# V in memory of its own and transposed early, both experts behind the output projection, output transposes last

## What is computed

```python
def _L0_attn_ref(q_x, ln1_w, ...):                 # q_x = layernorm(x)
    xn = _ln(q_x, ln1_w, ln1_b)
    q, k, v = (heads(xn @ w + b) for w, b in ...)  # 16 heads of 16
    fq = jax.nn.elu(q) + 1.0
    fk = jax.nn.elu(k) + 1.0
    kv = jnp.einsum('bhnd,bhne->bnde', fk, v)      # per row, summed over heads
    qkv = jnp.einsum('bhnd,bnde->bhne', fq, kv)
    k_sum = fk.sum(axis=1)
    qk = jnp.einsum('bhnd,bnd->bhn', fq, k_sum)
    attn = qkv / (qk[..., None] + 1e-06)
    attn = attn.transpose(0, 2, 1, 3).reshape(b, n, c) @ wo + bo
    x = q_x + attn
    h = _ln(x, ln2_w, ln2_b)
    h = jax.nn.gelu(h @ fc_w + fc_b, approximate=False)
    return x + (h @ proj_w + proj_b)

def _L0_ffn_ref(x, gate_w, ...):                   # x = layernorm(...), 8 experts
    logits = x.mean(axis=1) @ gate_w.T + gate_b
    gates = softmax over the two largest logits of each batch
    expert_out = jax.nn.gelu(jnp.einsum('bsd,eod->beso', x, expert_w) + expert_b, approximate=False)
    return jnp.einsum('be,beso->bso', gates, expert_out)

x = x + _L0_attn_ref(_layernorm(x), ...)
x = x + _L0_ffn_ref(_layernorm(x), ...)
```

## Time and profile before

| | us |
|---|---|
| median of 3 runs | 1278.87 (1278.82 to 1278.89) |
| profiled execution | 1278.0 |
| its span in the trace | 1276.2 |
| PE busy | 1108.7 (87%) |
| PE loading weights | 816.2 (64%) |
| DVE busy | 782.9 (61%) |
| ACT busy | 530.4 (42%) |
| POOL busy | 190.8 (15%) |
| mean granted TensorE clock | 0.884 |

### The profile page before, as it was taken

The page is one execution under the profiler, slowest core; times in us unless marked ns, Lnnn a source line. Parts: engine busy times, 40 slices in busy tenths (PEclk is TensorE's granted clock), DMA queues, the critical chain, the costliest instruction groups (busy, mean ns, idle before and its releaser), DMA issues.

```text
span 1276.2 us, 22032 instructions
## 1 busy us (share of the span) xinstructions
PE 1108.7 (87%) x7272; PEld 816.2 (64%) x7272; DVE 782.9 (61%) x1692; ACT 530.4 (42%) x835; POOL 190.8 (15%) x113
## 2 busy tenths in 40 slices
PE   6646988979797989999997989999999989795946
PEld 3444766757575858686775758586767667583723
DVE  2465566565757586666756676766666674646333
ACT  2413443534444444536353454536363444231322
POOL 1011202020111212120301112121203012111000
PEclk9757897979797989989897989899897989797969
DMA  4966656383737475665737473656658374311013
GB/s 161 187 143 157 116 140 149 104 180 95 173 98 173 104 165 115 173 148 153 168 121 173 114 172 116 160 128 173 148 147 174 125 165 106 102 55 53 17 66 116
DMA packets 242518, 170.21 MB, mean 133 GB/s; under 512 B 177040, under 2 KB 218256, under 8 KB 240144
## 3 DMA queue, kind: packets, MB, share of 16 engines
q1 hardware_dynamic: 235792, 158.80, 52.3%
q10 hardware_dynamic: 6656, 10.50, 2.4%
HBM read 93.75 MB, written 75.50 MB: 133 GB/s over the span
## 4 chain that ended last, share of the span: by engine, by line
PE 48%; issue 23%; DVE 14%; ACT 7%; DMA 3%; SPq 2%; POOL 1%; DVEq 1%; ACTq 0%; POOLq 0%
PE pq L963 13%; PE pj L949 10%; PE ps L925 7%; PE pq L869 5%; PE pt L934 4%; PE pt L857 3%; DVE nd L727 2%; DVE acc L818 2%; DVE am L700 1%; DVE hn L631 1%; ACT am L513 1%; DVE stat L621 1%; DMA scratch_nd<-ot 1%; DMA ot<-scratch_v 1%; SPq L366 1%
## 5 line engine op out<-in xcount | busy, mean ns | idle before, releaser
L716 DVE TENSOR_TENSOR hidden<-xhT,hidden 128x512 fp32r<-128x512 f32 x128 | 96.6, 755 | 224.0 <-ACT hidden L541 224.0
L963 PE MATMUL pq<-hT,w_fc 128*128 128x512 f32 x768 | 225.4, 433 | 9.4 <-DVE hT L723 5.2
L540 ACT ACTIVATE xhT<-pq,col 128x512 f32<-128x512 f32 x128 | 88.0, 688 | 323.1 <-PE pq L963 322.9
L949 PE MATMUL pj<-w_pj,hidden 128*128 128x256 f32 x1536 | 214.1, 288 | 0.7 <-DVE hidden L716 0.7
L949 PEld LDWEIGHTS pj<-w_pj,hidden 128*128 128x128 f32 x1536 | 191.6, 189 | 18.6 <-issue 9.8
L925 PE MATMUL ps<-kq 48*128 48x128 f32 x1024 | 155.7, 436 | 24.0 <-DVE am L700 14.7
L963 PEld LDWEIGHTS pq<-hT,w_fc 128*128 128x128 f32 x768 | 149.0, 207 | 41.3 <-issue 7.7
L700 DVE TENSOR_TENSOR am<-ps,mask 128x512 f32<-128x512 f32 x256 | 164.1, 682 | 17.4 <-PE ps L925 17.1
L925 PEld LDWEIGHTS ps<-kq 48*128 48x128 f32 x1024 | 133.8, 329 | 61.1 <-issue 36.9
L869 PE MATMUL pq<-zT,w_e 128*128 (+1 forms) x256 | 119.4, 614 | 11.8 <-DMA b_e<-in_eb 7.3
L458 POOL TENSOR_TENSOR rs<-var,mhalf 128x4 f32<-128x4 f32 x16 | 18.1, 1132 | 571.2 <-DVE var L744 571.2
(11 more groups left out here) (117 smaller groups left out, 1399.3 us busy)
## 6 DMA issues: line engine op xcount, KB each, us to landing
kq<-scratch_q SPq DMA_DIRECT2D x192, 128.0 KB, 3.7
kq<-scratch_k SPq DMA_DIRECT2D x192, 128.0 KB, 4.5
scratch_q<-hidden SPq DMA_DIRECT2D x32, 512.0 KB, 4.6
scratch_k<-hidden SPq DMA_DIRECT2D x32, 512.0 KB, 6.1
scratch_nd<-ot SPq DMA_DIRECT2D x16, 1024.0 KB, 3.9
nd<-scratch_nd SPq DMA_DIRECT2D x48, 256.0 KB, 3.3
x_sb<-in_x SPq DMA_DIRECT2D x16, 512.0 KB, 4.7
scratch_v<-feat_v ACTq DMA_DIRECT2D x16, 512.0 KB, 2.8
```

Of the source, the lines that this page charges most:

```text
L540: nc.scalar.activation(gelub[:, u], pq[u][:, :], ACT.Gelu, bias=b_fc[:, m:m + 1])
L716: nc.vector.tensor_tensor(hidden[:, m % SLOTS, 1], gelub[:, u], hidden[:, m % SLOTS, 0].bitcast(f32), ALU.subtract).then_inc(S["rest_ready ...
L949: last = nc.tensor.matmul(pj[u][:, D * s:D * (s + 1)], hidden[:, m % SLOTS, a, lo:lo + P], w_pj[:, b, m], start=False, stop=end)
L963: last = nc.tensor.matmul(pq[m % 2][:, :], w_fc[:, b, c, P * m:P * (m + 1)], hT[:, a, c], start=(n == 0), stop=(n == len(order) - 1))
```

## The change

- V is loaded into `vd`, a buffer of its own of 128 partitions, in which partition 8d + 2j + b holds dimension d of block (j, b). `VL` no longer waits for the store of `ot`; it waits until PE has read the last V, and stands second among SP's loads of a pass. To make room, `x2_sb` has one slot in place of two.
- V's transposes are 8 of 128 x 128 in place of 16 with 64 rows, and `VT` stands ahead of `N`, `D2` and `A2` in the pass.
- `F1` moves from ahead of `N` to behind `R`, next to `F3`. The DVE part of the second expert becomes a stage `F4` behind `H`; `FX` follows it.
- `F2` stands last in the pass, behind `B9`, and its transposes go into `pj`. `JA`, which empties `pj`, moves from the end of the pass to right behind `J7`.
- `E` moves behind `J7` in a full pass. The matmuls of zeros are gone: the first real matmul into each `pj` bank starts the accumulation.

```diff
-X2RING = 2
+X2RING = 1
...
-FULL = ["L", "XS", "M1", "K0", "J2", "Y", "M2", "DS", "M3", "Z", "D1", "M4", "VL", "XL", "X", "E", "J7", "F1", "N", "D2", "K1", "A2", "F3",
-        "FX", "R", "VT", "F2", "B0", "H", "B9", "JA"]
-HEAD = ["L", "XS", "M1", "K0", "J2", "Y", "M2", "DS", "M3", "Z", "D1", "M4", "VL", "XL", "E", "X", "J7", "G", "N", "D2", "K1", "F1", "A2",
-        "F3", "FX", "R", "VT", "F2", "B0", "H", "B9", "JA"]
+FULL = ["L", "XS", "M1", "VL", "K0", "J2", "Y", "M2", "DS", "M3", "Z", "D1", "M4", "XL", "X", "J7", "JA", "E", "VT", "N", "D2", "K1", "A2",
+        "R", "F1", "F3", "B0", "H", "F4", "FX", "B9", "F2"]
+HEAD = ["L", "XS", "M1", "VL", "K0", "J2", "Y", "M2", "DS", "M3", "Z", "D1", "M4", "XL", "E", "X", "J7", "JA", "G", "VT", "N", "D2", "K1", "A2",
+        "R", "F1", "F3", "B0", "H", "F4", "FX", "B9", "F2"]
...
-    stages(["XS", "C1", "J2", "C2", "Z", "C3", "C4", "XL", "J7", "E", "F1", "F3", "FX", "F2", "JA"], 18, [])
+    stages(["XS", "C1", "J2", "C2", "Z", "C3", "C4", "XL", "J7", "JA", "E", "F1", "F3", "F4", "FX", "F2"], 18, [])
...
+        vd = sb("vd", [P, H * HALF])
-        vd = ot
...
                 if p.stage == "VL":
                     wait("v_out", at("v_out"))
-                    wait("nd_out", at("nd_out"))
+                    for u in range(2):
+                        wait(f"pt_full{u}", at(f"pt_full{u}"))
...
-                if p.stage == "F3":
+                if p.stage == "F4":
                     for m in range(NC):
 
-                        wait(f"pq_free{m}", at(f"pq_free{m}", 1))
+                        wait(f"pq_free{m}", at(f"pq_free{m}"))
                         wait("acc_ready", at("acc_ready", m))
...
                 if p.stage == "VT":
                     wait("v_in", at("v_in"))
-                    rows, n = vd[0:NQ * HD].rearrange("p h t -> p (h t)"), NQ * HD
                     for u in range(2):
                         wait(f"pt_free{u}", at(f"pt_free{u}"))
-                        pe.sem_inc(held, 1)
-                        for g in range(HG):
-                            group = rows[:, P * HG * u + g:P * HG * (u + 1):HG]
-                            last = nc.tensor.transpose(pt[u][:, n * g:n * (g + 1)], group, ident[0:n, 0:n])
+                        for g in range(HG // 2):
+                            last = nc.tensor.transpose(pt[u][:, P * g:P * (g + 1)], vd[:, HG // 2 * u + g::HG], ident[:, :])
                         last.then_inc(S[f"pt_full{u}"], 1)
...
-                            nc.tensor.matmul(pj[u][:, :], zero[:, :], zero[:, :].unsqueeze(1).broadcast_to([1, 4, P]), start=True, stop=False)
...
-                                                        start=False, stop=end)
+                                                        start=(m == 0 and n == 0 and s == 0), stop=end)
...
                 if p.stage == "F2":
                     wait("acc_ready", at("acc_ready"))
                     for u in range(2):
-                        wait(f"pt_free{u}", at(f"pt_free{u}"))
+                        wait(f"pj_free{u}", at(f"pj_free{u}"))
```

More of the change, by code:

```diff
@@ L74 @@
 INC = {
[L75 to L78, removed]
+    "pt_full0": {"W1": 1, "WS": 1, "X": 1, "D2": 1, "VT": 1, "H": 1, "G": 1},
+    "pt_free0": {"W1": 1, "WS": 1, "X": 1, "D2": 1, "VT": 1, "H": 1, "G": 1, **rounds("pt_free0")},
+    "pt_full1": {"X": 1, "D2": 1, "VT": 1, "H": 1},
+    "pt_free1": {"X": 1, "D2": 1, "VT": 1, "H": 1, **rounds("pt_free1")},
     "pq_full0": {"D2": 1, "F1": 1, "F3": 1, **rounds("pq_full0")},
@@ L102 @@
     "pool_ready": {"G": 1}, "logit_ready": {"G": 1}, "gexp_ready": {"G": 1}, "gate_ready": {"G": 1},
-    "acc_ready": {"P": 1, "F1": 2, "F3": 2},
+    "acc_ready": {"P": 1, "F1": 2, "F4": 2},
     "out_stored": {"P": 16, "F2": 16},
@@ L161, in walk @@
     late = ["XS", "J2", "Z", "E"]
-    last = ["XL", "F1", "F3", "FX", "F2"]
+    last = ["XL", "F1", "F3", "F4", "FX", "F2"]
     def without(names, *out):
@@ L407, in run @@
                     for u in range(2):
-                        wait(f"pt_free{u}", at(f"pt_free{u}", 1))
+                        wait(f"pj_free{u}", at(f"pj_free{u}", 1))
                     sp.dma_start(out_t[p.t], out_sb[:, :, :]).then_inc(S["out_stored"], 16)
@@ L418, in _ @@
             nc.gpsimd.memset(mhalf[:, :], -0.5).then_inc(const_done, 1)
-            nc.gpsimd.memset(vd[:, :, :], 0.0).then_inc(const_done, 1)
+            nc.gpsimd.memset(vd[:, :], 0.0).then_inc(const_done, 1)
             nc.gpsimd.memset(vb[:, :, :], 1.0).then_inc(const_done, 1)
@@ L520, in run @@
                         wait(f"pt_full{u}", at(f"pt_full{u}", 1))
[L521 to L522 removed]
+                        src = pt[u][:, :].rearrange("p (g d j) -> p j g d", d=HD, j=2 * NQ)
+                        dst = vb[:, :, :].rearrange("p (j g) e -> p j g e", j=2 * NQ)[:, :, HG // 2 * u:HG // 2 * (u + 1), 0:HD]
                         nc.scalar.activation(dst, src, ACT.Identity).then_inc(S[f"pt_free{u}"], 1)
@@ L832, in run @@
                     for u in range(2):
-                        wait(f"pt_full{u}", at(f"pt_full{u}", 1))
+                        wait(f"pj_full{u}", at(f"pj_full{u}", 1))
                         o = out_sb[:, 2 * u:2 * u + 2]
-                        nc.vector.tensor_tensor(o, pt[u][:, :].rearrange("p (s d) -> p s d", d=D), o,
-                                                ALU.add).then_inc(S[f"pt_free{u}"], 1)
+                        nc.vector.tensor_tensor(o, pj[u][:, :].rearrange("p (s d) -> p s d", d=D), o,
+                                                ALU.add).then_inc(S[f"pj_free{u}"], 1)
             walk(dve, run)
@@ L845, in _ @@
                 pe.wait_ge(w_in[n], 16)
+            features_copied = []
             def run(p):
@@ L896, in run @@
                     transposes(xhat)
+                    features_copied[:] = [at(f"pt_free{c}", 1) for c in range(NC)]
                 if p.stage == "D2":
-                    copied(0)
+                    for c in range(NC):
+                        wait(f"pt_free{c}", features_copied[c])
                     for j in (4, 5, 0, 1, 2, 3):
@@ L1051, in run @@
                                 lo = P * (2 * u + s)
-                                last = nc.tensor.transpose(pt[u][:, D * s + P * m:D * s + P * (m + 1)],
+                                last = nc.tensor.transpose(pj[u][:, D * s + P * m:D * s + P * (m + 1)],
                                                            acc[:, m, lo:lo + P], ident[:, :])
-                        last.then_inc(S[f"pt_full{u}"], 1)
+                        last.then_inc(S[f"pj_full{u}"], 1)
             walk(pe, run)
```

12 lines of the change are left out of this document (5 added, 7 removed).

## The result

The changed kernel takes 1286.3 us (median of four runs, 1284.61 to 1286.83) against 1278.88 (1278.82 to 1279.81): 1.0059 times, with a 95% interval of 1.0043 to 1.0076. It is slower by 0.6%. Two later comparisons of the same pair gave 1.0079 [1.0061, 1.0096] and 1.0066 [1.0041, 1.009]. The predicted time was 1287.

A forecast was written before the change was run, and what follows sets the result against it. PE bounds the rounds, a DVE chain the end of a pass. Full passes +11.2, gate +1.6, early -4.1, passes 16 and 17 +1.4, pass 18 -1.8 sum to +8.3 us: 1287 predicted, range 1271 to 1297; slower had 0.62.

The forecast's parts named there:

- Start of N: DVE's reciprocal and split, bound in full passes by the landing of `nd`: 6.36 us after I, a gain of 0.26.
- I: The first issue of the loads of `nd` in a pass, from which the prediction counts its times.
- the mark (I + 5.4): Sign of being wrong: DVE's N starting 5.4 us after I with `out_sb`'s load behind the `nd` loads.
- N to the end of `hn`: DVE's stretch from reciprocal to `hn`, without an expert in it: 20.68 us, as in an early pass.
- `hn` to U: From `hn` to the next pass's first product (U): 5.2 us on DVE, then 2.0 of output transposes; 4.04 before.
- Passes with the gate: Three passes where the addition `JA` delays the gate's sum on DVE: +0.5 us each, +1.6 together.
- The rounds: PE-bound stretch of a pass: without the matmuls of zeros 0.53 us less; V's earlier loads make nothing wait.
- Early passes and tail: Five early passes, `nd` landing at 5.4: -4.1 us; passes 16 and 17: +1.4; pass 18: -1.8.
- the clock holds: Faster rival: PE's clock stays at 1.00 through the end of a pass, 21 us less, 1266; chance 0.10.
- The rule of the Trainium skill: Transposes don't count as PE-busy like matmuls; low stretch begins as now, ends later: sum +14, time 1292.
- Cancelling: No-change rival: output transposes at the high clock, or `nd` landing at 4.3; either gives 1275 to 1279; chance 0.15.
- The wait for V: Faster rival: half of ACT's 29.3 us of waits behind V's load set the end: sum -6.4, 1272; chance 0.13.

## Why the prediction was right

**How near.** The mechanism and the sign were right. That 1287 stands so close to 1286.3 is in part luck: term by term the traces differ from the forecast by -3.0, +0.1, -0.5, +1.9, +0.4, -1.2 and +0.6 us (in the order of the table), which adds up to -1.7 only.

**What bounds the kernel.** Right: a chain of DVE sets the end of a pass. PE lost 33 us of busy time, and the time rose.

**Start of N.** The gain was taken too small: N came at I + 5.3 to 6.1, not 6.36. The single row of pass 17 was the late end of a scatter; the same pass after the change has 5.79. Pass 13 had 5.34, which is past the mark (I + 5.4) that the prediction had set as a sign of being wrong; the mean of the six is 5.67. The choice of the row by its neighbour in the queue was right in kind: with the same load behind them the `nd` loads land later than in the early passes 3 to 6 (4.5 to 4.8), and the run with that load moved shows it. This is the term that was off most, 0.7 us in each of six passes, 4 us in sum.

**N to the end of `hn`.** 20.68 was predicted; the six full passes have 20.68 to 20.71. V's early transposes and both experts are hidden behind it, as was said.

**`hn` to U.** 5.2 + 2.0 predicted, 7.23 to 7.25 measured in five of the full passes. Pass 10 has 11.84: the pause described in the last section stands there, and it grew from 3.9 to 4.6 us against the other passes, which is +0.7 that the sum didn't have. The parts are a little different (5.63 to the output transposes, 1.62 from there): F1 took 0.87 for both, not 1.0; DVE's idle time behind ACT (0.74) wasn't in the sum; and the transposes are 1.97 long but the product starts 1.62 after their start, since the two overlap. These cancel, which is luck too. The wait of ACT that causes the 0.74 was missed because the stage `F3` inherited `acc_ready` from `F1`: a wait whose text doesn't change, but whose producer moved from I + 6.2 to I + 26.1.

**Passes with the gate.** +3.3 against +3.2, by two errors that cancel. N came at I + 7.4 to 7.8 (7.97 predicted), which is 1.4 us less over the three passes, and N to the end of `hn` was set at the 20.68 of an early pass and is 21.1 to 21.4, which is 1.9 us more. Before, this stretch took 24.5 to 25.6. The prediction puts the gain down to the first expert alone; V's early load has a part in it that it doesn't name, for with V alone the stretch is already down to 23.5 to 23.7.

**The rounds.** -7.6 against -8.0 in the traces (-5.5 and -6.5 in the two later ones), and 0.43 to 0.52 us a pair in the run with zeros against 0.53. V's loads in front of K0's cost nothing that can be seen. Single passes scatter by 1 to 1.5 us either way, so only the sum says something. What makes them scatter was not looked into.

**Early passes and tail.** -2.5 against -2.0, but not evenly: passes 3 to 6 gained 3.5 us in sum, since N came at I + 4.5 to 4.8 and not at 5.4, and pass 2 lost 1.0, with N at I + 6.31. The tail had -1.2 against -1.8. Passes 16 and 17 cost 4.4, not 2.5. They have `hn` to U in nearly the full length (7.1), while N to the end of `hn` got 1.4 to 1.6 us shorter. In pass 16 N came at I + 7.45 in this trace and at 5.57 in another of the same kernel, so 1.9 us of the 4.4 is scatter, and that other trace (+3.5 for both passes) stays inside the prediction's bounds of 0 to 1.9 net a pass.

**The clock.** The forecast held the low stretch to be as long as before. It was shorter: stretches of half a microsecond with a granted clock under 0.75, from 90 to 1190 us, sum to 230 us before and 208 after (213 and 217 in the two later traces). In the pass shown the transposes of `hn` ran at the high clock (1.09 us where the earlier trace rows has 1.97), the clock fell in the stretch from 608 to 610, and the output transposes and the start of the product behind them were at 0.50. Counted from I, the low stretch began 3.6 us later than before in this pass and ended at the same I + 35. So both ends of the rival "the clock holds" are seen: it held longer, but in a piece during which PE waits for DVE anyway, and the output transposes were not in it. The rule of the Trainium skill ("TensorE: Matmul & The Clock Gate", Part 4: PE-mode transpose) as the prediction applied it, a low stretch that begins as before and lasts longer, did not come: 1292 was too much. That transposes as such don't hold the clock isn't contradicted, since the clock did fall ahead of them; no run here separates it. The run with V's part alone has 209 us too, with the output transposes at their old place, so nothing shows the shorter sum to be the work of their move.

**Rivals.** The clock holds: see above, no gain. Cancelling: its second half, early landing, came by a third (0.7 of 2 us). The wait for V: worth 2 us when its removal ran alone, where the rival had 14.7.

## What to carry over

Before moving work out of a stage, list who reads its semaphore by count: a later stage that waits for "all so far" waits for the moved piece too. Of the pieces between the last normalisation and the product that everything waits for, put only those ahead that this product reads; what is moved there "because the engine idles" takes its producers' waits along. And a good order shows its worth only when the piece behind it is right too: by the traces, the accumulation's move was worth 0.3 us a pass with one neighbour and 1.2 with another.

## What the runs showed of the hardware

The landing of a load depends on what is issued behind it. In the full passes of the two kernels that ran side by side, DVE starts on `nd` 4.6 to 5.0 us after the first issue with nothing behind the three loads, and 5.3 to 6.0 with a load of 512 KB right behind. DVE's wait for them is 42.3 us in sum in the first case and 48.0 in the second. Over all traces of this case single passes overlap: with the load behind, 54 full passes have 4.9 to 6.4 us (mean 5.66), and without it 12 have 4.6 to 5.1 (mean 4.84).

The other transfer may not have to be on the same queue. In pass 2 nothing stands behind the `nd` loads on SP's queue, in any kernel but the one before, and DVE still starts late in most of them: 4.9 to 6.5 us after the first issue (mean 6.0), where passes 3 to 6 have 4.5 to 5.3 (mean 4.9). In the changed kernel it is 6.31, counted from 101.32. There ACT issues V's store of 512 KB 1.8 us after that first issue, where in passes 3 to 6 it does so only after DVE has started. Timelines of ACT and DVE, pass 2 of the changed kernel:

```profile
103.09 0.37 ACTq L500 DMA_DIRECT2D scratch_v<-feat_v  x1
107.63 3.35 DVE L728 RECIPROCAL nd<-nd 128x512 f32<-128x512 f32 x1 [13.12 <-DMA nd<-scratch_nd]
```

No run moves this store, so that it is the cause is argued, not shown.

Between passes 10 and 11 PE stands for 4 us without a releaser in the trace. There the kernel's outer hardware loop (passes 7 to 10, then 11 to 14) goes back to its start. Timeline of PE, pass 10 of the changed kernel:

```profile
682.68 1.97 PE L1052 MATMUL pj<-ident,acc 128*128 128x128 f32 x8 [2.26 <-DVE acc L819]
688.90 2.92 PE L963 MATMUL pq<-hT,w_fc 128*128 128x512 f32 x6 [4.25 <-issue]
```

It is there in all kernels (4.17 before). It isn't there behind pass 14, which ends the same inner loop and where the outer loop is left: `hn` to U is 7.24 there, as in the other full passes. The trace has one packet of the kind `instruction` on queue q8 (16 KB) inside the pause, at 685.2 us, and none on that queue between 516.2 us and this one; the kernel before has one at 683.5, in a pause that ends at 687.12. So a fetch of instructions for the jump back may be the cause. It was not tested. In the kernels with the first product moved the pause stands in the rounds of pass 11 (43 to 46 us where others have 37 to 40).
